# Layer three of a four-layer attention stack: the softmax rows transposed by one DMA per item instead of by the tensor engine

## The reference

```python
def _cross_attention(q_in, kv_in, wq, bq, wk, bk, wv, bv, wo, bo, bias_k, bias_v):
    ...
    qh = (q_in @ wq + bq).reshape(b, q_len, H, K)
    kh = (kv_in @ wk + bk).reshape(b, t, H, K)
    vh = (kv_in @ wv + bv).reshape(b, t, H, K)
    kh = jnp.concatenate([kh, jnp.broadcast_to(bias_k, (b, 1, H, K))], axis=1)
    vh = jnp.concatenate([vh, jnp.broadcast_to(bias_v, (b, 1, H, K))], axis=1)
    scale = jnp.sqrt(jnp.asarray(K, q_in.dtype))
    logits = jnp.einsum('bqhk,bthk->bhqt', qh, kh) / scale
    weights = jax.nn.softmax(logits, axis=-1)
    ctx = jnp.einsum('bhqt,bthk->bqhk', weights, vh).reshape(b, q_len, H * K)
    return ctx @ wo + bo
...
    h = _layer_norm(x, ln1_scale, ln1_offset)
    x = res + _cross_attention(h, xf_1, wq1, bq1, wk1, bk1, wv1, bv1, wo1, bo1, bias_k1, bias_v1)
    res = x
    h = _layer_norm(x, ln2_scale, ln2_offset)
    x = res + _cross_attention(h, xf_2, wq2, bq2, wk2, bk2, wv2, bv2, wo2, bo2, bias_k2, bias_v2)
    h = _layer_norm(x, ln_mlp_scale, ln_mlp_offset)
    h = jax.nn.gelu(h @ w_fc1 + b_fc1, approximate=False) @ w_fc2 + b_fc2
    return x + h
```

## Time and profile before

| | us |
|---|---|
| median of 3 runs | 2162.23 |
| lowest and highest | 2161.11, 2163.47 |
| the profiled execution, its own time | 2160.24 |
| span of its trace | 2158.5 |
| PE busy | 1932.7 (90%) |
| DVE busy | 1080.9 (50%) |
| ACT busy | 956.9 (44%) |
| POOL busy | 707.7 (33%) |

### The profile page before, as it was taken

The page is one execution under the profiler, slowest core; times in us unless marked ns, Lnnn a source line. Parts: engine busy times, 40 slices in busy tenths (PEclk is TensorE's granted clock), DMA queues, the critical chain, the costliest instruction groups (busy, mean ns, idle before and its releaser), DMA issues.

```text
span 2158.5 us, 39293 instructions
## 1 busy us (share of the span) xinstructions
PE 1932.7 (90%) x16097; PEld 1644.8 (76%) x16097; DVE 1080.9 (50%) x1979; ACT 956.9 (44%) x2550; POOL 707.7 (33%) x819
## 2 busy tenths in 40 slices
PE   6788887898999999999999999999989788878798
PEld 4566665786888888888888888888867666657587
DVE  4444544544444444455554444445443577686743
ACT  4244333333444444343434443444434467666633
POOL 3322222402232413234233241323321367666500
PEclk9899998999999999999999999999999899999899
DMA  3000001100000000000001010000020000000000
...
DMA packets 28035, 38.45 MB, mean 18 GB/s; under 512 B 1344, under 2 KB 19408, under 8 KB 27856
## 3 DMA queue, kind: packets, MB, share of 16 engines
q1 hardware_dynamic: 27856, 35.95, 5.2%
...
...
## 4 chain that ended last, share of the span: by engine, by line
PE 77%; DVE 10%; ACT 8%; issue 3%; POOL 1%; DMA 0%; ACTq 0%; SPq 0%; DVEq 0%; POOLq 0%
PE ps_high L196 40%; PE ps_four L196 7%; PE ps_four L2613 5%; PE ps_four L2633 5%; PE ps_four L2622 2%; PE ps_four L2417 2%; PE ps_high L2509 2%; PE ps_high L2400 1%; ACT l_pt L1717 1%; PE ps_four L2425 1%; PE ps_four L2539 1%; PE ps_high L2438 1%; ACT l_pt L1759 1%; DVE l_sm L2134 1%; PE ps_four L2549 1%
## 5 line engine op out<-in xcount | busy, mean ns | idle before, releaser
L1813 ACT ACTIVATE l_prob<-ps_four,l_mx 128x129 f32<-128x129 f32 x512 | 181.7, 368 | 565.3 <-DVE l_mx L2169 565.3
L1605 POOL TENSOR_TENSOR l_prob<-l_prob,l_mx 128x516 f32<-128x516 f32 x128 | 134.4, 1050 | 723.2 <-DVE l_mx L2176 723.2
L196 PE MATMUL ps_high<-ctxT,l_wk 128*128 128x512 f32 x768 | 211.9, 412 | 0.0
L196 PE MATMUL ps_high<-l_hT,l_wq 128*128 128x512 f32 x768 | 209.8, 408 | 0.0
L196 PEld LDWEIGHTS ps_high<-l_wo,l_ao 128*128 128x128 f32 x1536 | 196.3, 189 | 14.0 <-DVE l_ao L2188 3.1
L196 PE MATMUL ps_high<-l_wo,l_ao 128*128 128x256 f32 x1536 | 202.3, 281 | 1.9 <-DVE l_ao L2188 1.9
L196 PE MATMUL ps_high<-l_wv,ctxT 128*128 128x512 f32 x768 | 201.8, 398 | 1.8 <-ACT l_qT L1794 1.4
L1571 POOL TENSOR_TENSOR l_sm<-l_sm,l_mask 128x1024 f32<-128x1024 f32 x64 | 150.3, 2370 | 119.8 <-DVE l_sm L2134 119.6
L196 PEld LDWEIGHTS ps_high<-l_wv,ctxT 128*128 128x128 f32 x768 | 143.0, 189 | 44.0 <-ACT l_qT L1794 10.3
L196 PEld LDWEIGHTS ps_high<-ctxT,l_wk 128*128 128x128 f32 x768 | 137.2, 192 | 23.1
L196 PEld LDWEIGHTS ps_high<-l_hT,l_wq 128*128 128x128 f32 x768 | 134.6, 188 | 22.9
...
## 6 DMA issues: line engine op xcount, KB each, us to landing
l_staging<-in_L_xattn_wv SPq DMA_DIRECT2D x8, 512.0 KB, 3.6
l_staging<-in_L_xattn_wk SPq DMA_DIRECT2D x8, 512.0 KB, 3.6
l_staging<-in_L_xattn_wq SPq DMA_DIRECT2D x8, 512.0 KB, 4.0
l_staging<-in_L_xattn_wo SPq DMA_DIRECT2D x8, 512.0 KB, 3.5
ctx_tok<-in_ctx SPq DMA_DIRECT2D x8, 256.0 KB, 3.3
x_tok<-in_x SPq DMA_DIRECT2D x4, 512.0 KB, 5.5
l_raw_w<-in_L_xattn_mlp_w SPq DMA_DIRECT2D x2, 1024.0 KB, 7.5
l_staging<-in_L_xattn_w_fc SPq DMA_DIRECT2D x4, 512.0 KB, 4.1
```

What stands on the lines that cost most here:

```text
L196: ins = e.matmul(out, a, b, start=start and i == 0, stop=stop and i == 2, skip_group_check=not check)
L1605: e.tensor_tensor(pr[:, :, 0:S + 1], pr[:, :, 0:S + 1], mx[:, 3, :].unsqueeze(2).to_broadcast([P, GB, S + 1]), ALU.mult).then_inc(sem("poo ...
L1813: ins = e.activation(pr.t[:, b, 0:S + 1], banks[b // 2].t[:, (b % 2) * (S + 2):(b % 2) * (S + 2) + S + 1], ACT.Exp, bias=mx[:, 1, b:b + 1] ...
```

## The change

In layer three the probabilities are no longer transposed by PE. ACT copies the 32-bit rows as pairs of 16-bit words into two planes (`l2_planes`, one for each half of the word), SP starts one DMA that transposes the eight 128 x 128 blocks of 16-bit words (`l2_tr`), and DVE puts the two transposed planes together again in `l2_probT` (`l2_merge`). In the diff the three stages are given with their code, `l2_tr` from SP's program, `l2_planes` from ACT's and `l2_merge` from DVE's. Both plane buffers are single; to make room, `l2_qT` and `l2_kT` have one buffer in place of two. The order in a step is another: the values product comes last, its second half on DVE (`l2_rest`) and the output projection come in the step after it. The layer norms' transposes take bank 2 alone. Weights are loaded from ACT's queue in place of SP's, and `load_weights` has one more `yield` for each weight.

```diff
-L2_SLACK, L2_SPACE = 2, (230, 18)
+L2_SLACK, L2_SPACE = 2, (238, 18)
...
-        QT = self.ring("l2_qT", 2, [P, T], F32, scope)
-        KT = self.ring("l2_kT", 2, [P, GB, S + 2], F32, scope)
+        QT = self.ring("l2_qT", 1, [P, T], F32, scope)
+        KT = self.ring("l2_kT", 1, [P, GB, S + 2], F32, scope)
+        planes = [Slot(sb("l2_planes" + n, [P, 2, GB, S], U16)) for n in ("", "T")]
...
                 yield from pl.until(staging)
+                yield
                 pl.slot(staging, "l2_staging", k, at, hg)
...
         def transposes(n):
-            pl.bank(tr_ring, "l2_tr", n)
+            pl.emit("l2_planes", n, free=planes[0].freed if n == 0 else None)
+            pl.free("l2_prob", n, by=("act.l2_planes", n))
+            pl.emit("l2_tr", n, landed=self.dma("sp.l2_tr"), free=planes[1].freed if n == 0 else None)
+
+        def merge(n):
             pl.slot(PT, "l2_probT", n)
-            pl.emit("l2_tr", n)
-            pl.free("l2_tr", n)
-            pl.free("l2_prob", n, by=("full", "l2_tr", n))
+            pl.emit("l2_merge", n)
...
+        self.tr = self.banks(2)
...
             if 1 <= step <= N:
                 scores(step - 1)
+            if 3 <= step:
+                rest(step - 3)
             if step < N:
                 project(step, "q")
             if 1 <= step <= N:
                 normalise_rows(step - 1)
-            if 2 <= step <= N + 1:
-                values(step - 2)
-            if step >= N:
-                next(mlp)
-                next(mlp)
-            advance(weights_ahead, 1)
-            advance(norms_ahead, 4 if step < 12 else 2)
             if step < N:
                 project(step, "k")
-            project(step - 2, "v")
-            if 2 <= step <= N + 1:
-                output(step - 2)
-            if step >= N:
+            else:
                 next(mlp)
                 next(mlp)
             if 1 <= step <= N:
                 transposes(step - 1)
+            if 2 <= step:
+                merge(step - 2)
+            if 3 <= step:
+                output(step - 3)
+            advance(weights_ahead, 1 if step < N - 4 else 2)
+            advance(norms_ahead, 4 if step < 12 else 2)
+            project(step - 2, "v")
+            if step >= N:
+                next(mlp)
+                next(mlp)
+            if 2 <= step:
+                values(step - 2)
+        rest(N - 1)
+        output(N - 1)
...
+        def l2_tr(n):
+            f = pl.info["l2_tr", n]
+            q.wait_ge(*pl.done("act.l2_planes", n))
+            q.wait_ge(*(pl.done("dve.l2_merge", n - 1) if n else pl.event(f["free"])))
+            e.dma_start(self.planes[1][:].rearrange("p i b t -> p (i b) t"), self.planes[0][:].rearrange("p i b t -> p (i b t)"),
+                        transpose=True).then_inc(sem("sp.l2_tr"), 16)
...
+        def l2_planes(n):
+            q.wait_ge(*pl.done("pool.l2_norm:n", n))
+            q.wait_ge(*(pl.event(pl.info["l2_tr", n - 1]["landed"]) if n else pl.event(pl.info["l2_planes", n]["free"])))
+            e.activation(self.planes[0][:].rearrange("p i b t -> p b t i"),
+                         use["l2_prob", n].t[:, :, 0:S].bitcast(U16).rearrange("p b (t i) -> p b t i", i=2), ACT.Copy).then_inc(
+                             sem("act.l2_planes"), 1)
...
+        def l2_merge(n):
+            pt = use["l2_probT", n]
+            q.wait_ge(*pl.event(pl.info["l2_tr", n]["landed"]))
             q.wait_ge(*pl.event(pt.before))
-            e.tensor_copy(pt.t[:], bk.t).then_inc(bk.slot.empty, 1)
+            e.tensor_copy(pt.t[:].bitcast(U16).rearrange("p (b t i) -> p b t i", b=GB, i=2),
+                          self.planes[1][:].rearrange("p i b t -> p b t i")).then_inc(sem("dve.l2_merge"), 1)
```

86 lines of the change are left out of this document (40 added, 46 removed).

## The result

The changed kernel takes 2279.02 us (median of four runs, 2274.71 to 2284.71) against 2162.49 us before (2161.11 to 2163.47): the ratio is 1.0541, with a 95% interval of 1.0510 to 1.0571. It is 5.4% slower, where 2143 us was forecast.

A forecast was written before the change was run, and what follows sets the result against it. PE was taken to bound layer three's attention. From 2160.2 us, 62.5 came off for transposes and longer fourth items; 36 for late weights, 3 and 4 were added: 2140.7, predicted as 2143 us, range 2105 to 2260.

The forecast's parts named there:

- what it adds: Layer three's chain replacing PE's transposes: planes on ACT 1.35 us, DMA 4.6, merge on DVE 1.25; in time, costing nothing.
- Planes: 1024 elements on ACT: ACT's copy of one item's rows into the planes: 1.35 us, between 1.2 and 2.4.
- the transfer's room: Time the transposing DMA may take before the single plane buffer delays the next planes: 5.95 us.
- Rival 2: Layer three's DMA slightly too long for its single buffer, planes plus DMA over 7.3 us: 2172 to 2219 us, chance 0.18.
- the other ring: Loop of planes, DMA and next planes through the single buffer; sets the step if the DMA exceeds 5.95 us.
- PE's step: PE's time per item in layer three's attention, scores to scores: 7.38 us, where it was 7.81.
- The longer fourth item: One item of four took 8.05 us, waiting for the queries' bank; the new order removes this, 7.5 us.
- the waits for the norms' bank: Layer norms' transposes waited 14.1 us for the values' bank; with bank 2 alone: 0, between -14 and +10.
- The smaller terms of +3 and +4: +3 us for weight loads sharing DMA engines with the transposes; +4 for the last item's uncovered chain.
- The DMA: Transposing transfer of 256 KB, SBUF to SBUF, per item: 4.6 us, between 3.0 and 6.1, in time at no cost.
- Rival 3: DMA far too long, its blocks one behind another or in smaller pieces: about 2730 us, chance 0.14.
- The weights: At seven head-group ends, `wo` halves on POOL delay the last rows; PE waits 5.15 us for the merge: 36 us.

The follow-up runs named there:

- run 1: The change with ACT's planes copy as two instructions of 512 elements, one plane each with dense writes, in place of one: 2130.65 us.
- run 11: run 5 with the planes' copy as one instruction of 1024 elements, the plane as the outer loop, in place of two: 2092.63 us.
- run 2: The change without the added yield in the weight loads, the planes' copy as in the change: 2242.51 us.
- run 5: The change with both edits of run 1 and run 2, planes copied one at a time and no added yield: 2097.39 us.
- run 8: The change with the planes copied on DVE, one plane at a time, and the previous item's merge ahead of them: 2143.28 us.
- run 12: run 5 with the planes copied in pairs of neighbouring elements, by four instructions of 256 elements, one per batch: 2094.51 us.
- run 10: The kernel before with only the new step order and bank 2 for the norms; transposes on PE and weights as before: 2136.64 us.
- run 6: run 1 with the transposing DMA issued twice in a row, the second after the first has landed: 2196.76 us.

## Why the prediction was wrong

**The step that failed** is the first of "what it adds": "Planes: 1024 elements on ACT. No row has this shape. From below, twice the 512-element row from PSUM, 1.2 us; from above, four times the 256-element row from SBUF, 2.4 us. I take 1.35". Measured: 4.84 us. Both rows used as bounds were of dense 32-bit writes. I counted elements and left out the pattern, which the diff shows (`p i b t -> p b t i` on the output). So the upper bound bounded nothing. The price of this one term, with all else equal, is 2279.0 - 2130.7 = 148 us by run 1 and 2242.5 - 2092.6 = 150 us by run 11 against run 2. Had the order been dense, the planes would have taken 1.06 us in one instruction or 1.24 in two, at or below my lower bound of 1.2.

**What hung on it.** I compared planes plus DMA only with the transfer's room, and looked for ACT as a bound nowhere. The ring through ACT's queue (planes, evacuation, exponentials, reciprocal, rows) was missing from the working; by the timeline it sets the step once the planes take over 4.1 us. Rival 2 had the other ring and the right sign ("planes plus DMA against 7.3 us"; they are 4.85 + 3.1 here), but its time of 2172 to 2219 was made with planes within my bounds (its second sum is also off: a step of 7.95 us gives 2172 + 0.4 x 128 = 2223).

Inside layer three the change and run 1 are 141.9 us apart. The step of 8.12 in place of 7.34 us accounts for the 41.7 us of items 3 to 56. Items 76 to 127 lose 54.1, since items 117, 121 and 125 are longer by 17.8 together. The first three items lose 6.1. And 40.0 us lie in the 20 items of the norms' region, 2.0 each. The busy table shows two causes there; first three stretches at item 57 of the change, then the region of the change (columns as in the earlier trace rows, the granted clock third from the end), then that of run 1:

```profile
1012.00:1018.00 6.00, 2.55 (x15) 2.25 (x15) 0.72 (x1) 5.20 (x2) 2.69 (x5) 0.57 0.00 0
1018.00:1022.00 4.00, 3.13 (x14) 2.63 (x13) 2.41 (x4) 1.22 (x2) 0.00 (x0) 0.50 0.36 70
1022.00:1026.00 4.00, 4.00 (x15) 3.52 (x15) 0.69 (x1) 0.51 (x2) 0.00 (x0) 0.50 0.00 0
996.00:1209.00 213.00, 175.71 (x999) 151.16 (x998) 101.89 (x222) 166.84 (x252) 67.58 (x89) 0.90 0.18 40
```

```profile
954.00:1127.00 173.00, 161.22 (x998) 141.56 (x997) 96.93 (x221) 98.96 (x271) 68.31 (x89) 0.98 0.24 49
```

PE first waits for evacuations that stand on ACT behind the planes. The rows of waits of the same two stretches:

```profile
PE ps_high L2703 <- ACT l_pbT L1863: 11.3, 3, 3.9
PE ps_four L2502 <- ACT l_staging L1699: 6.0, 2, 5.1
```

```profile
PE ps_high L2704 <- ACT l_pbT L1864: 2.2, 3, 0.7
PE ps_four L2503 <- ACT l_staging L1699: 2.2, 2, 1.3
```

All waits of PE in the region add up to 37 us in the change and 12 in run 1, 25 more. Behind such a wait the granted clock is at its lower level: 0.57 in the stretch with PE busy for 2.55 of 6 us, and 0.50, which is 1.2 GHz, in the 8 us behind it, with PE busy all the time in the last 4. A mean of 0.90 over 213 us means 43 us at the lower level; 0.98 over 173 us means 7. Work done at half speed costs half of that time: (43 - 7) / 2 = 18 us, an estimate. 25 + 18 = 43, of 40.0 measured; some of the time at the lower level lies in the waits themselves, so 18 is rather too high. In this region the long instruction on ACT is paid for twice: in PE's wait, and in slower work behind it.

**PE's step.** 7.38 us forecast, 7.31 to 7.41 in runs 1, 5, 8, 11 and 12. The longer fourth item is gone in run 10 (mean step 7.78), though items 3 to 56 and 76 to 127 gain 3 us by it together, where 7.5 were forecast for all. From run 10 to run 5 the step falls by 0.45 us, 0.43 forecast. In the whole run, all that separates run 5 from run 10, which is the transposes with their chain, the single buffers and the weights' queue, brings 39 us, though, in place of 55 (run 10 is 23.0 us under its kernel before, run 5 is 62.0): in items 56 to 76 only 1.9 us come back of 20 x 0.45, and the first three items get 2.8 us longer. PE does not set the pace there. On the other side the order brings 23 us in place of 7.5; 8.3 of these are the waits for the norms' bank, which I had put at 0 with -14 as one end. The two errors cancel: 39 + 23 = 62, and 55 + 7.5 = 62.5. That they do is luck. The smaller terms of +3 and +4, which run 5 has in it too, are not seen: from the last item's scores to the end of the span it is 605.5 us before and 606.1 in the change, and the weights' share of the DMA engines was not measured by itself.

**The DMA.** 4.6 us forecast between 3.0 and 6.1, 3.1 measured; it was mis-sized, but the direction and the conclusion (in time, costs nothing) hold once the planes are fast. The upper bound had the number of packets right and their time wrong. The weights' packets are in a queue of their own now, so the transposes have 150672 + 12352 - 27856 = 135168, or 1056 each, where 1024 were assumed. By the queues' shares they take some 21 ns each, an estimate from the rows of both pages, where I had used the 64 ns of the old queue's mix. The rule of the Trainium skill that the prediction weighed, in "Advanced Engine Details and Errata", section "X-Bar Transpose (TRN2)", that transposing DMAs are as fast as regular ones, agrees with the trace: 3.1 us against 3.0 for the plain 256 KB. Rival 3's 10.5 us, an estimate from the Trainium skill's price of one block ("VectorE: DVE Perf Modes", section "The three transpose paths"), is not borne out: eight blocks together land in 3.1 us. Run 6 confirms the room.

**The weights.** 36 us forecast, 36.5 by the medians from the change to run 2, and 33.3 from run 1 to run 5 (35 and 29 by the ratios). POOL does the halves of `wo` ahead of the rows, as the timeline at 641.82 to 646.53 shows, and ACT waits 4.23 us for the rows. So far it is as forecast, but the wait that PE pays is another one. The prediction has PE wait 5.15 us for the merge, ahead of the values product. In run 1, with the late weights and the short planes, PE does not wait for the merge in any item (its weight load does once, for 0.3 us). The first end of a head group in run 1, PE's two waits and then the timeline and a stretch behind it:

```profile
PE ps_four L2648 <- issue: 3.5, 1, 3.5
PE ps_high L197 <- POOL l_wq L1513: 1.0, 1, 1.0
```

```profile
636.38 1.04 POOL L1609 TENSOR_TENSOR l_prob<-l_prob,l_mx 128x516 f32<-128x516 f32 x1
...
637.62 0.19 POOL L1602 COPY l_kT<-columns 128x8 f32<-128x8 f32 x1
...
637.91 2.07 PE L2648 MATMUL ps_four<-l_kT,l_qT 128*128 128x130 f32 x8 [3.48 <-issue]
```

```profile
638.00:640.00 2.00, 2.00 (x9) 2.00 (x10) 0.43 (x1) 1.19 (x3) 0.00 (x0) 0.50 0.07 15
```

PE waits ahead of the next scores. They need the added key, which POOL copies into `l_kT` behind the late rows. The profile names no releaser, but the kernel's scores wait for this copy, and at six of the seven ends the scores begin 0.10 us after it ends (637.81 and 637.91 here). These six waits are 2.5 to 3.9 us; at item 63 it is `wq` that PE waits for, 3.1 us. Behind this pause the scores' eight records take 2.07 us where 1.06 is usual, with the granted clock at 0.50, its lower level of 1.2 GHz.

This path does not go through the DMA, so the price should hang on its length less than forecast (25 us at 3.0, 45 at 5.9), and it does: run 6 makes the transfer some 3 us longer, PE then does wait for the merge, and the ends and the steps behind them grow by 10 us in all where 21 had been expected. With a DMA of 3.0 us I had worked out 25 us. In run 1 the seven steps themselves are 32.7 us longer than in run 5 and the seven behind them 6.3, while three other steps are shorter by 4.5. So the 36 us came out right by luck: too long a DMA, and a wait in the wrong place.

**The merge**: 1.25 us forecast, a median of 0.695 measured, in the change and in run 8. It has room in either case.

With the planes as in run 1 the kernel takes 2130.7 us; the forecast's sum with a DMA of 3 us would have been 2132. That they agree is in part luck, by the errors named above that cancel. Two things failed: the planes' number, which with the missing ring makes the whole distance to the result, and the wait given for the late weights, which does not show in the sum.
